# VectorE's general path rolled into a loop, and its flag made earlier

## The chip, the cores and the metric

One core of one Trainium2 chip runs the kernel. The metric is the device time of one execution in microseconds; the kernel before takes 160.34 us (median of 3 runs, 160.16 to 160.55).

## What is computed

For each of 128 graphs with 128 nodes and 128 features, `x` holds the node features and `adj` the integer kind of each edge. Two layers follow each other:

```python
# layer 1; rels(a, r) is (a == r) as 0.0 or 1.0
h = x @ W.T
vals_r = (h + b_r) * sigmoid(h @ Wg.T + bg_r)       # W, Wg, b, bg for each way
y = sum(rels(adj, r) @ vals_r for r in 2..40)       # forward
y += sum(rels(adj.T, r) @ vals_r for r in 2..40)    # backward
y += rels(adj.T, 1) @ vals_1                        # loop
x = layernorm(x + relu(y))
# layer 2
y = sum(rels(adj, r) @ x @ weight[r] for r in 1..4) + bias
x = layernorm(x + y)
```

The drawn `adj` holds only 0 and 1. So of the 40 relations of layer 1 and the 4 of layer 2 only relation 1 has edges.

## The kernel before

**The fast path.** It takes `adj` to be 0 or 1 everywhere. The 128 graphs are 32 groups of four. Each group is one tile of 128 x 512, and a software pipeline runs over the groups. TensorE projects (`project`), sums over neighbours (`loop_sum`), forms the messages (`messages`) and multiplies them by the weight (`message_weights`). ScalarE seeds PSUM, takes the sigmoid, copies messages, scales the second norm's outputs and looks at every tile of `adj` (`look`, whose sums land in `seen_sum`). VectorE forms the products and residual sums and the moments of both norms. GpSimd applies the first norm and takes inverse roots of variances by a power. SP (SyncE) issues loads of `x` and its transpose and all stores. GpSimd issues the loads of `adj` and its transpose.

**The tail.** The last five groups, `LAST` = 27 to `LAST + 4` = 31, are written out by hand below the loops (lines 1075 to 1106 for VectorE, 601 to 615 for TensorE, 771 to 782 for ScalarE, 433 to 439 for GpSimd, 323 to 332 for SP). On VectorE the order of calls in that list is the order of the work. A variance made by `last_variance(q)` (L905) releases a power on GpSimd (L410). That power releases the scaling of group q by ScalarE (L716) or by VectorE (`last_norm2`, L1015), and the scaled tile releases SP's store (L301). The last group is handled in halves (`half_...`; variances L984, powers L405).

**The flag.** `find_odd` reduces `seen_sum` (L1020) and compares (L1023). Its comparison gives one value per partition, which says whether an edge kind other than 0 and 1 was seen. TensorE adds these over partitions with a matmul against ones (L614), and VectorE copies the sum as an integer to `flag` (L1103). VectorE's reduction stands behind the statistics of group `LAST + 2`, TensorE's matmul behind all other matmuls, and the copy just ahead of the last variance.

**The general path.** Every engine ends with `general` (L272): it waits for `flag_ready`, loads the flag into a register (L274) and branches (L275). With the flag at 0 it jumps over the whole general path. Only with a flag above 0 would it compute everything again, for any `adj`, in 16 pairs of groups. For this input each engine waits, loads, compares and jumps. SP then waits at L353 until all stores have landed, and all engines meet at the end (L80).

The general path of TensorE and of ScalarE already has a loop over the two groups of a pair. That of VectorE is written out twice, by a Python `for` at L1141:

```python
            def general_pair(pair):
                dve.wait_ge(gadj_in, (pair + 1) * 32)
                for half_ in range(2):
                    g = pair * 2 + half_
```

Of the kernel before, what the change touches and what calls it, by code (L numbers as in the profile page):

```python
# [5 lines left out]
F32 = mybir.dt.float32  # L6
# [3 lines left out]
ALU = mybir.AluOpType  # L10
# [3 lines left out]
P = 128  # L14
B = 128
GB = 4
# [3 lines left out]
EPS = 1e-5  # L20
# [32 lines left out]
FWD, BWD, LOOP = range(3)  # L53
RSQRT_MAGIC = float(0x5F3759DF)
NEWTON = 3
CHAIN = 1 + 2 * (1 + 5 + 3 * NEWTON)


def exists(q):
# [18 lines left out]
def build(nc, x, x_t, adj, adj_t, w_in, w_loop_t, wg_loop_t, gate_bias, consts,  # L78
          w_rel_t, wg_rel_t, b_rel, bg_rel, w_msgs, rel_ids, out):
    with ExitStack() as ctx:  # L80
        def sb(name, shape, dt):
            return ctx.enter_context(nc.sbuf_tensor(name, shape, dt))
# [61 lines left out]
        gsum = sb("gsum", [P, W], F32)  # L144
        gx1 = sb("gx1", [P, W], F32)
        gmsg = sb("gmsg", [P, GB, MSGS * P], F32)
        gstat = sb("gstat", [P, GB, 6], F32)
        gmv = sb("gmv", [P, GB, 2], F32)
        gtiny = sb("gtiny", [P, 4, GB], F32)
        worst = sb("worst", [P, 1], F32)  # L150
        odd = sb("odd", [P, 1], F32)
# [92 lines left out]
        def half_columns(p):  # L244
            return slice(2 * p * P, 2 * (p + 1) * P)
# [14 lines left out]
        def batch(b):  # L260
            return slice(b * P, (b + 1) * P)
# [189 lines left out]
        def _(pe):  # L451
# [105 lines left out]
            def inject(q):  # L557
                pe.wait_ge(consts_in, 16)
                await_x1(q)

                pe.wait_ge(vals_done, q + 1)
                for b in range(GB):
                    nc.tensor.matmul(y_of(q, b, 1), ident, x1[:, q % X1_RING, batch(b)],
                                     start=b == 0, stop=False, skip_group_check=True)

            def message_weights(q):
                if exists(q):
                    if q == 0:
                        pe.wait_ge(w1_mid, 6)

                    if q in INJECTED:
                        pe.wait_ge(vals_done, q + 1)
                    else:
                        await_count(pe, z_done, q)
                    pe.wait_ge(msgt_done, q + 1)
                    for b in range(GB):
                        last = nc.tensor.matmul(y_of(q, b, 1), msg_t[:, q % 2, batch(b)], w1[:, :],  # L577
                                                start=q not in INJECTED, stop=True,
                                                skip_group_check=q in INJECTED)
                    last.then_inc(y_done, 1)  # L580

            for t in range(GROUPS):
# [20 lines left out]
            message_weights(GROUPS - 3)  # L603
            messages(GROUPS - 2)
            inject(GROUPS - 2)
            message_weights(GROUPS - 2)
            half_messages(0)
            half_messages(1)
# [1 line left out]
            half_message_weights(0)  # L610
            half_inject(1)
            half_message_weights(1)
            pe.wait_ge(odd_ready, 2)
            nc.tensor.matmul(aux_ps[0:1, 2 * P:2 * P + 1], odd[:, :], ones[:, :], start=True, stop=True)\  # L614
                .then_inc(odd_count, 1)

            def relation(step, ways):
                pe.wait_ge(rel_vals, step)
# [201 lines left out]
        def _(dve):  # L820
# [137 lines left out]
            def half_variance1(p):  # L958
                q = GROUPS - 1
                dve.wait_ge(bn1_done, q + 1 + p)  # L960

                dve.wait_ge(nmr_done, q - 1)
                m2 = stats[:, q % STATS_RING, p, :].rearrange("p (i k) -> p i k", k=3)[:, :, 2]
                ts(var1[:, q % 2, 2 * p:2 * p + 2], m2, 1.0 / P, EPS, ALU.mult, ALU.add).then_inc(mean_done, 1)
# [21 lines left out]
            def second_sum(q):  # L986
                dve.wait_ge(y_done, q + 1)
                dve.wait_ge(x1_done, q + 1)

                await_count(dve, out_done, q - Z_RING + 1)  # L990
                tt(z_sb[:, q % Z_RING, :], y_ps[:, :], x1[:, q % X1_RING, :], ALU.add).then_inc(z_done, 1)  # L991
# [89 lines left out]
            half_first_stats(1)  # L1081
            second_stats(LAST + 1, 1)
            half_variance1(1)
            second_sum(LAST + 2)
            last_variance(LAST + 1)
            half_norm1(0)
            second_stats(LAST + 2, 0)
            half_norm1(1)
            second_stats(LAST + 2, 1)
            odd_steps = find_odd()  # L1090
            next(odd_steps)
            second_stats(LAST + 3, 0)
            last_variance(LAST + 2)
            next(odd_steps, None)
            second_stats(LAST + 3, 1)
            last_norm2(LAST + 2, (0, 1))
            last_variance(LAST + 3)
# [1 line left out]
            last_norm2(LAST + 2, (2, 3))  # L1099
            half_variance2(0)  # L1100
            second_stats(LAST + 4, 1)
            dve.wait_ge(odd_count, 1)
            nc.vector.tensor_copy(flag[:, :], aux_ps[0:1, 2 * P:2 * P + 1]).then_inc(flag_ready, 1)  # L1103
            half_variance2(1)
            last_norm2(LAST + 4, (0, 1))
            last_norm2(LAST + 4, (2, 3))
# [1 line left out]
            def vals_and_masks(step, half_, ways, r, number):  # L1108
                dve.wait_ge(rel_gates, step)
                for way in ways:  # L1110
                    source = LOOP if r is None else way
                    column = bass.ds(2 * RELS if r is None else r + way * RELS, 1)
                    stt(gvals_t[:, way, :], gh[:, source, :], gb[:, column], ggate[:, way, :], ALU.add, ALU.mult)
                for way in ways:
                    edges = adjt_sb[:, half_, :] if way == FWD else adj_sb[:, half_, :]
                    last = ts(gmask[:, way, :], edges, number, None, ALU.is_equal)
                last.then_inc(rel_vals, 1)

            def normalise(dst, src, chain):
                var, y, yy, w = (gtiny[:, i, :] for i in range(4))  # L1120
                for b in range(GB):
                    last = nc.vector.bn_stats(gstat[:, b, :], src[:, batch(b)])
                chain(last)
                nc.vector.tensor_copy(worst[:, :], ones[:, :])
                for b in range(GB):
                    last = nc.vector.bn_aggr(gmv[:, b, :], gstat[:, b, :])
                chain(last)
                chain(ts(var, gmv[:, :, 1], EPS, None, ALU.add))
                chain(ts(y.bitcast(I32), var.bitcast(I32), -0.5, RSQRT_MAGIC, ALU.mult, ALU.add))
                for _ in range(NEWTON):  # L1130
                    chain(tt(yy, y, y, ALU.mult))
                    chain(stt(w, yy, -0.5, var, ALU.mult, ALU.mult))
                    chain(stt(y, w, 1.5, y, ALU.add, ALU.mult))
                for b in range(GB):
                    last = ts(dst[:, batch(b)], src[:, batch(b)], gmv[:, b, 0:1], y[:, b:b + 1],
                              ALU.subtract, ALU.mult)
                chain(last)

            def general_pair(pair):
                dve.wait_ge(gadj_in, (pair + 1) * 32)  # L1140
                for half_ in range(2):  # L1141
                    g = pair * 2 + half_
                    steps = [0]

                    def chain(ins):
                        steps[0] += 1
                        ins.then_inc(gchain, 1)
                        dve.wait_ge(gchain, g * CHAIN + steps[0])

                    first = g * (RELS + 1) + 1  # L1150
                    vals_and_masks(first, half_, (BWD,), None, 1.0)
                    dve.wait_ge(rel_product, first)
                    nc.vector.tensor_copy(gsum[:, :], bank[3]).then_inc(rel_added, 1)
                    with dve.Fori(0, RELS) as r:
                        vals_and_masks(first + 1 + r, half_, (FWD, BWD), r, gids[:, bass.ds(r, 1)])
                        dve.wait_ge(rel_product, first + 1 + r)
                        tt(gsum[:, :], bank[3], gsum[:, :], ALU.add).then_inc(rel_added, 1)
                    dve.wait_ge(rel_added, first + RELS)
                    dve.wait_ge(gx_in, (g + 1) * 32)
                    chain(stt(gsum[:, :], gsum[:, :], 0.0, x_sb[:, 0, :], ALU.max, ALU.add))  # L1160
                    normalise(gx1, gsum, chain)
                    for k in range(MSGS):
                        last = ts(gmask[:, k, :], adjt_sb[:, half_, :], float(k + 1), None, ALU.is_equal)
                    last.then_inc(gmasks_ready, 1)
                    dve.wait_ge(gy_done, g + 1)
                    chain(tt(gsum[:, :], y_ps[:, :], gx1[:, :], ALU.add))
                    for b in range(GB):
                        last = tt(gsum[:, batch(b)], gsum[:, batch(b)], b1, ALU.add)
                    chain(last)
                    normalise(out_sb[:, 0, :], gsum, chain)  # L1170
                    assert steps[0] == CHAIN
                    nc.vector.tensor_copy(worst[:, :], ones[:, :]).then_inc(gout_ready, 1)
                    dve.wait_ge(gout_st, (g + 1) * 16)

            general(dve, general_pair)


# [46 lines left out]
```

## Time and profile before

| | us |
|---|---|
| median of 3 runs | 160.34 |
| profiled execution | 159.43 |
| its span in the trace | 157.3 |
| PE, DVE, ACT, POOL busy | 149.0, 138.5, 128.1, 113.5 |

The span runs from the first to the last instruction of the trace. The profiled execution's own time is 2.1 us longer, and lies 0.9 us under the median of the unprofiled runs. PE is TensorE, DVE VectorE, ACT ScalarE, POOL GpSimd and SP SyncE. A name with a q behind it is that engine's sequencer: it handles waits, register loads, branches and DMA issues. Durations of single instructions are in ns, all other times in us.

### The profile page before, as it was taken

The numbers are of one execution on the slowest core, as the hardware profiler recorded it, in microseconds if no ns is written. First come the engines' busy times: TensorE is split into PE (matmuls) and PEld (weight loads), VectorE is DVE, ScalarE is ACT, GpSimd is POOL, SyncE is SP. The second block draws the span as 40 slices with busy tenths as digits, with TensorE's granted clock in tenths as the row PEclk, the third lists the DMA queues.
The fourth block names the chain that finished last, engine by engine and source line by source line (L and its number), as shares of the span: only waits on it lengthen the run. The fifth ranks groups of instructions, "written<-read, shape, count | busy, mean of one in ns | idle before, by whom it ended". The sixth has DMA issues, their size and how long they took to land.

```text
span 157.3 us, 3862 instructions
## 1 busy us (share of the span) xinstructions
PE 149.0 (95%) x1055; PEld 138.7 (88%) x1055; DVE 138.5 (88%) x567; ACT 128.1 (81%) x293; POOL 113.5 (72%) x221
## 2 busy tenths in 40 slices
PE   6999999999999999999999999999999999999920
PEld 3698999999999999999999999999999999999920
DVE  1459599799999999999999999999999999999870
ACT  3579888769888888889988888889988888869940
POOL 1318878847877778779877778778877776867760
PEclk9999999999999999999999999999999999999996
DMA  3999999997899998999899999999989862341243
GB/s 129 307 391 400 403 395 391 404 312 247 234 310 277 295 287 300 311 301 321 284 292 311 308 290 277 305 276 299 323 308 295 250 206 77 108 162 67 109 164 140
DMA packets 19320, 42.75 MB, mean 272 GB/s; under 512 B 2144, under 2 KB 2784, under 8 KB 19296
## 3 DMA queue, kind: packets, MB, share of 16 engines
q1 hardware_dynamic: 14400, 25.76, 48.2%
q0 software_dynamic: 4608, 16.52, 32.9%
q8 instruction: 9, 0.15, 0.4%
q10 hardware_dynamic: 288, 0.20, 0.4%
q14 instruction: 15, 0.12, 0.2%
HBM read 34.08 MB, written 8.39 MB: 270 GB/s over the span
## 4 chain that ended last, share of the span: by engine, by line
PE 80%; DMA 5%; DVE 4%; issue 3%; SPq 2%; POOL 2%; POOLq 0%; DVEq 0%
PE hg_ps L473 31%; PE loop_ps L488 17%; PE msg_ps L553 16%; PE y_ps L577 16%; DMA xt_sb<-x_t_dram 5%; POOL last_rstd L410 1%; SPq L293 1%; DVE last_stats L1004 1%; POOL last_rstd L405 1%; PE aux_ps L553 1%; SPq L298 1%; DVE x L974 1%; DVE s_sb L948 0%; DVE out_sb L1015 0%; DVE z_sb L991 0%
## 5 line engine op out<-in xcount | busy, mean ns | idle before, releaser
L473 PE MATMUL hg_ps<-w_all,xt_sb 128*128 128x256 f32 x256 | 60.8, 381 | 0.2
L388 POOL TENSOR_SCALAR x<-s_sb,rstd,nmr 128x128 f32<-128x128 f32 x114 | 49.7, 448 | 3.3
L473 PEld LDWEIGHTS hg_ps<-w_all,xt_sb 128*128 128x128 f32 x256 | 46.2, 190 | 6.0 <-DMA xt_sb<-x_t_dram 0.8
L379 POOL TENSOR_TENSOR rstd<-var,power 128x4 f32<-128x4 f32 x31 | 32.0, 1033 | 20.9 <-DVE var L913 18.4
L716 ACT ACTIVATE out_sb<-z_sb,rstd 128x128 f32<-128x128 f32 x108 | 36.9, 392 | 0.5 <-DVE rstd L885 0.5
L674 ACT ACTIVATE hg_ps<-gate_b 128x1024 f32<-128x1024 f32 (+1 forms) x32 | 31.9, 1000 | 2.6 <-DVE vals L921 1.9
L683 ACT ACTIVATE gate<-hg_ps 128x512 f32<-128x512 f32 x32 | 19.0, 595 | 17.5 <-PE hg_ps L473 17.5
L488 PE MATMUL loop_ps<-vals,adj_sb 128*128 128x128 f32 x248 | 33.0, 276 | 0.2
L577 PEld LDWEIGHTS y_ps<-w,msg_t 128*128 128x128 f32 x240 | 31.3, 191 | 1.5
L577 PE MATMUL y_ps<-w,msg_t 128*128 128x128 f32 x240 | 31.8, 275 | 0.0
L488 PEld LDWEIGHTS loop_ps<-vals,adj_sb 128*128 128x128 f32 x248 | 30.5, 192 | 0.7 <-issue 0.5
L553 PE MATMUL msg_ps<-adjt_sb,x 128*128 128x128 f32 x232 | 30.7, 275 | 0.0
L553 PEld LDWEIGHTS msg_ps<-adjt_sb,x 128*128 128x128 f32 x232 | 28.2, 192 | 0.2 <-DMA adjt_sb<-adj_t_dram 0.2
L931 DVE SCALAR_TENSOR_TENSOR s_sb<-loop_ps,x_sb 128x512 f32<-128x512 f32 x31 | 21.4, 689 | 6.3 <-PE loop_ps L488 3.2
L936 DVE BATCH_NORM_STATS2 stats<-s_sb 128x6 f32<-128x256 f32 x62 | 25.5, 427 | 0.0
L1004 DVE BATCH_NORM_STATS2 stats<-z_sb 128x6 f32<-128x256 f32 x54 | 22.9, 427 | 0.0
L921 DVE TENSOR_TENSOR vals<-hg_ps,gate 128x512 f32<-128x512 f32 x32 | 21.7, 680 | 1.2 <-ACT gate L683 1.2
L741 ACT ACTIVATE seen<-adj_sb,half 128x512 bf16<-128x512 f32 x32 | 22.7, 710 | 0.0
L991 DVE TENSOR_TENSOR z_sb<-y_ps,x 128x512 f32<-128x512 f32 x30 | 20.4, 680 | 1.1 <-PE y_ps L577 1.1
L693 ACT ACTIVATE msg_t<-msg_ps 128x512 f32<-128x512 f32 x29 | 16.8, 580 | 0.0
L362 POOL DMA_DIRECT2D adj_sb<-adj_dram x15 | 9.3, 623 | 4.7 <-DMA xt_sb<-x_t_dram 2.6
L369 POOL DMA_DIRECT2D adjt_sb<-adj_t_dram x16 | 10.1, 631 | 0.0
(93 smaller groups left out, 119.8 us busy)
## 6 DMA issues: line engine op xcount, KB each, us to landing
xt_sb<-x_t_dram SPq DMA_DIRECT2D x32, 256.0 KB, 4.2
x_sb<-x_dram SPq DMA_DIRECT2D x32, 256.0 KB, 4.2
adjt_sb<-adj_t_dram POOLq DMA_DIRECT2D x16, 512.0 KB, 5.1
out<-out_sb SPq DMA_DIRECT2D x32, 256.0 KB, 3.3
adj_sb<-adj_dram POOLq DMA_DIRECT2D x15, 512.0 KB, 5.2
raw<-adj_dram SPq DMA_DIRECT2D x1, 256.0 KB, 3.7
adj_sb<-adj_dram POOLq DMA_DIRECT2D x1, 256.0 KB, 5.8
const_sb<-consts_dram SPq DMA_DIRECT2D x1, 192.0 KB, 6.2
```

What stands on the lines that cost most here:

```text
L379: nc.gpsimd.tensor_tensor(r, var1[:, q % 2, :], power[:, :], ALU.pow).then_inc(rstd1_done, 1)
L388: done = nc.gpsimd.tensor_scalar(x1[:, q % X1_RING, batch(b)], s_sb[:, q % S_RING, batch(b)], r[:, b:b + 1], n[:, b:b + 1], ALU.mult, ALU.add)
L473: last = nc.tensor.matmul(hg_ps[:, q % 2, b, :], xt_sb[:, q % XT_RING, batch(b)], w_gate, start=False, stop=True, skip_group_check=True)
L488: last = nc.tensor.matmul(loop_ps[:, batch(b)], adj_sb[:, spot, batch(b)], vals[:, q % 2, batch(b)], start=True, stop=True)
L553: last = nc.tensor.matmul(msg_of(q)[:, batch(b)], x1[:, q % X1_RING, batch(b)], adjt_sb[:, spot, batch(b)], start=True, stop=True)
L577: last = nc.tensor.matmul(y_of(q, b, 1), msg_t[:, q % 2, batch(b)], w1[:, :], start=q not in INJECTED, stop=True, skip_group_check=q in IN ...
L674: nc.scalar.activation(hg_ps[:, q % 2, 0:graphs, :], gate_b[:, None, :].broadcast_to([P, graphs, 2 * P]), ACT.Copy).then_inc(seeded, 1)
L716: last = nc.scalar.activation(out_sb[:, q % OUT_RING, batch(b)], z, ACT.Copy, scale=r)
L741: nc.scalar.activation(seen[:, :], adj_sb[:, 2 * spot + q % 2, :], ACT.Square, bias=half[:, 0:1], accum_out=seen_sum[:, q:q + 1]).then_inc ...
L921: tt(vals[:, q % 2, :].rearrange("p (b n) -> p b n", b=GB), hg_ps[:, q % 2, :, 0:P], gate[:, q % 2, :].rearrange("p (b n) -> p b n", b=GB) ...
L936: got = nc.vector.bn_stats(stats[:, q % STATS_RING, p, :], s_sb[:, q % S_RING, 2 * p * P:2 * (p + 1) * P].rearrange("p (i n) -> p n i", i=2))
L1004: got = nc.vector.bn_stats(into, z.rearrange("p (i n) -> p n i", i=2))
```

## The change

On VectorE the two groups of the general path become a loop in the instruction stream, and `normalise` takes statistics of two interleaved graphs per instruction, drops the aggregation and adds the bias in one instruction. In all VectorE's general path has 111 instructions for 231. None of these runs for this input.

In the tail, the reduction goes right behind `half_variance1(1)`, the last variance of the first norm, and the comparison behind `second_sum(LAST + 2)`. TensorE's matmul for the flag goes between `inject(GROUPS - 2)` and `message_weights(GROUPS - 2)`, and VectorE's copy to `flag` behind `half_norm1(1)`. Scratch tiles of the general path shrink.

```diff
@@ TensorE
             messages(GROUPS - 2)
             inject(GROUPS - 2)
+            pe.wait_ge(odd_ready, 2)
+            nc.tensor.matmul(aux_ps[0:1, 2 * P:2 * P + 1], odd[:, :], ones[:, :], start=True, stop=True)\
+                .then_inc(odd_count, 1)
             message_weights(GROUPS - 2)
...
             half_message_weights(1)
-            pe.wait_ge(odd_ready, 2)
-            nc.tensor.matmul(aux_ps[0:1, 2 * P:2 * P + 1], odd[:, :], ones[:, :], start=True, stop=True)\
-                .then_inc(odd_count, 1)
@@ VectorE
             half_variance1(1)
+            odd_steps = find_odd()
+            next(odd_steps)
             second_sum(LAST + 2)
+            next(odd_steps, None)
             last_variance(LAST + 1)
             half_norm1(0)
             second_stats(LAST + 2, 0)
             half_norm1(1)
+            dve.wait_ge(odd_count, 1)
+            nc.vector.tensor_copy(flag[:, :], aux_ps[0:1, 2 * P:2 * P + 1]).then_inc(flag_ready, 1)
             second_stats(LAST + 2, 1)
-            odd_steps = find_odd()
-            next(odd_steps)
             second_stats(LAST + 3, 0)
             last_variance(LAST + 2)
-            next(odd_steps, None)
             second_stats(LAST + 3, 1)
...
             second_stats(LAST + 4, 1)
-            dve.wait_ge(odd_count, 1)
-            nc.vector.tensor_copy(flag[:, :], aux_ps[0:1, 2 * P:2 * P + 1]).then_inc(flag_ready, 1)
             half_variance2(1)
@@ VectorE, general path (jumped over)
             def general_pair(pair):
-                dve.wait_ge(gadj_in, (pair + 1) * 32)
-                for half_ in range(2):
+                with dve.Fori(0, 2) as half_:
+                    dve.wait_ge(gadj_in, (pair + 1) * 32)
                     g = pair * 2 + half_
...
             def normalise(dst, src, chain):
                 var, y, yy, w = (gtiny[:, i, :] for i in range(4))
-                for b in range(GB):
-                    last = nc.vector.bn_stats(gstat[:, b, :], src[:, batch(b)])
+                for p in range(2):
+                    last = nc.vector.bn_stats(gstat[:, p, :],
+                                              src[:, half_columns(p)].rearrange("p (i n) -> p n i", i=2))
                 chain(last)
-                nc.vector.tensor_copy(worst[:, :], ones[:, :])
-                for b in range(GB):
-                    last = nc.vector.bn_aggr(gmv[:, b, :], gstat[:, b, :])
-                chain(last)
-                chain(ts(var, gmv[:, :, 1], EPS, None, ALU.add))
+                m = gstat[:, :, :].rearrange("p c (i k) -> p (c i) k", k=3)
+                chain(ts(var, m[:, :, 2], 1.0 / P, EPS, ALU.mult, ALU.add))
...
-                    for b in range(GB):
-                        last = tt(gsum[:, batch(b)], gsum[:, batch(b)], b1, ALU.add)
-                    chain(last)
+                    by_graph = gsum[:, :].rearrange("p (b n) -> p b n", b=GB)
+                    chain(tt(by_graph, by_graph, b1[:, None, :].broadcast_to([P, GB, P]), ALU.add))
```

## Rows read from the trace of the kernel before

**Rows 1.** The page's chain that ended last, shares of the span by engine.

```profile
PE 80%; DMA 5%; DVE 4%; issue 3%; SPq 2%; POOL 2%; POOLq 0%; DVEq 0%
```

**Rows 2.** SP's stores (L301): the issue at 153.4, landings of 153:154, 152:153, 147:152.

```profile
L301 SPq DMA_DIRECT2D out<-out_sb x1: 1752/1752/1752, 153.4 to 153.4; - x1
DMA to landing us min/median/max: 3.5/3.5/3.5
...
DMA to landing us min/median/max: 3.7/3.7/3.7
...
DMA to landing us min/median/max: 2.0/2.0/2.0
```

**Rows 3.** Instruction fetches by queue (packets, MB, share): 153.1:153.4, 153.42:153.5, 154.6:154.75, 107.4:107.6.

```profile
q8 instruction: 1, 0.02, 35.1%
...
q14 instruction: 1, 0.01, 59.9%
...
q14 instruction: 1, 0.01, 16.6%
...
q8 instruction: 1, 0.02, 29.4%
```

**Rows 4.** SP's queue, packets, MB and share of 16 engines in 150:152.

```profile
q1 hardware_dynamic: 162, 0.30, 40.4%
```

**Rows 5.** SP's load issue (L293) and store issue (L301) in 107:109.

```profile
L293 SPq DMA_DIRECT2D xt_sb<-x_t_dram x1: 1202/1202/1202, 107.6 to 107.6; - x1
...
L301 SPq DMA_DIRECT2D out<-out_sb x1: 344/344/344, 107.2 to 107.2; - x1
```

**Rows 6.** L274 and L275: TensorE's load of the flag, branches of three engines.

```profile
L274 PEldq TENSOR_LOAD <-flag x1: 693/693/693, 151.5 to 151.5; - x1
...
L275 ACTq COMPARE_BRANCH  x1: 50/50/50, 152.4 to 152.4; - x1
L275 PEldq COMPARE_BRANCH  x1: 237/237/237, 152.7 to 152.7; - x1
...
L275 DVEq COMPARE_BRANCH  x1: 72/72/72, 153.7 to 153.7; - x1
```

**Rows 7.** The meeting at the end, L80: VectorE's drain.

```profile
L80 DVEq DRAIN  x1: 59/59/59, 156.6 to 156.6; - x1
```

**Rows 8.** Timeline of VectorE: start, duration, instruction.

```profile
145.63 0.15 DVE L964 TENSOR_SCALAR var<-stats 128x2 f32<-128x2 f32 x1
...
148.05 0.17 DVE L1020 TENSOR_REDUCE worst<-seen_sum 128x1 f32<-128x32 f32 x1
148.14 0.42 DVE L1004 BATCH_NORM_STATS2 last_stats<-hg_ps 128x6 f32<-128x256 f32 x1
148.48 0.15 DVE L905 TENSOR_SCALAR last_var<-last_stats 128x4 f32<-128x4 f32 x1
148.54 0.15 DVE L1023 TENSOR_SCALAR odd<-worst 128x1 f32<-128x1 f32 x1
148.60 0.42 DVE L1004 BATCH_NORM_STATS2 last_stats<-hg_ps 128x6 f32<-128x256 f32 x1
...
151.35 0.13 DVE L1103 CAST flag<-aux_ps 1x1 int32<-1x1 f32 x1
151.47 0.17 DVE L984 TENSOR_SCALAR last_var<-last_stats 128x2 f32<-128x2 f32 x1
```

**Rows 9.** Timeline of GpSimd from 148.7, idle time and its releaser in brackets.

```profile
148.71 1.01 POOL L410 TENSOR_TENSOR last_rstd<-last_var,power 128x4 f32<-128x4 f32 x1 [1.11 <-DVE last_var L905]
150.39 1.01 POOL L410 TENSOR_TENSOR last_rstd<-last_var,power 128x4 f32<-128x4 f32 x1 [0.68 <-DVE last_var L905]
151.37 1.36 POOL L405 TENSOR_TENSOR last_rstd<-last_var,power 128x2 f32<-128x2 f32 x2
```

**Rows 10.** Timeline of ScalarE's last look and of TensorE's last groups of matmuls.

```profile
144.91 0.19 ACT L741 ACTIVATION_READ_ACCUMULATOR seen<-adj_sb,half 128x1 f32 x1
...
149.78 0.61 PE L531 MATMUL hg_ps<-w,msg_t 128*128 128x128 f32 x4
150.32 0.19 PE L614 MATMUL aux_ps<-ones,odd 128*1 128x1 f32 x2
```

More of the change, by code:

```diff
@@ L55 @@
 NEWTON = 3
-CHAIN = 1 + 2 * (1 + 5 + 3 * NEWTON)
+CHAIN = 1 + 2 * (1 + 4 + 3 * NEWTON)
 def exists(q):
@@ L146, in build @@
         gmsg = sb("gmsg", [P, GB, MSGS * P], F32)
-        gstat = sb("gstat", [P, GB, 6], F32)
-        gmv = sb("gmv", [P, GB, 2], F32)
+        gstat = sb("gstat", [P, 2, 6], F32)
         gtiny = sb("gtiny", [P, 4, GB], F32)
@@ L1114, in vals_and_masks @@
                 for way in ways:
-                    edges = adjt_sb[:, half_, :] if way == FWD else adj_sb[:, half_, :]
-                    last = ts(gmask[:, way, :], edges, number, None, ALU.is_equal)
+                    edges = (adjt_sb if way == FWD else adj_sb)[:, bass.ds(half_, 1), :]
+                    last = ts(gmask[:, way, :], edges.rearrange("p o n -> p (o n)"), number, None, ALU.is_equal)
                 last.then_inc(rel_vals, 1)
@@ L1134, in normalise @@
                 for b in range(GB):
-                    last = ts(dst[:, batch(b)], src[:, batch(b)], gmv[:, b, 0:1], y[:, b:b + 1],
+                    last = ts(dst[:, batch(b)], src[:, batch(b)], m[:, b, 1:2], y[:, b:b + 1],
                               ALU.subtract, ALU.mult)
@@ L1161, in general_pair @@
                     normalise(gx1, gsum, chain)
+                    edges = adjt_sb[:, bass.ds(half_, 1), :].rearrange("p o n -> p (o n)")
                     for k in range(MSGS):
-                        last = ts(gmask[:, k, :], adjt_sb[:, half_, :], float(k + 1), None, ALU.is_equal)
+                        last = ts(gmask[:, k, :], edges, float(k + 1), None, ALU.is_equal)
                     last.then_inc(gmasks_ready, 1)
@@ L1173, in general_pair @@
                     dve.wait_ge(gout_st, (g + 1) * 16)
+                    nc.vector.tensor_copy(worst[:, :], ones[:, :])
             general(dve, general_pair)
```

## The prediction

> **What bounds the kernel now.** The page's chain comes first. It runs for 80% of the span through TensorE's matmuls [rows 1]. The change touches none of these; all of it lies behind 145.6 us of a span of 157.3. So I read the tail, from the end backwards. The last thing to happen is the landing of the last store: issued at 153.40, landed 3.5 us later, at 156.9, and the meeting of the engines ends 0.4 us behind that. The reader should see two oddities in the rows of the stores [rows 2]. The last issue occupied SP for 1752 ns, and the two last stores took 3.7 and 3.5 us to land where the four before them took 2.0. So the tail holds about 1.5 us that is neither computing nor a store's ordinary time.
>
> The queues say what stood there [rows 3]. A share of 16 engines turned back into the time of one packet (35.1% of 16 x 0.30 us) gives 1.68 us for a fetch of 16 KB of instructions that began between 153.1 and 153.4; one of 8 KB at 153.42 to 153.50 took 59.9% of 16 x 0.08 = 0.77 us, and one of 8 KB at 154.60 to 154.75 took 0.40 us. They follow the jumps over the general path [rows 6]: TensorE branches at 152.7 and the 16 KB fetch begins 0.4 us later; ScalarE at 152.4 and VectorE at 153.7, and an 8 KB fetch begins 1.0 us after each. I take these three pairings as right; nothing but the times ties them.
>
> That a 16 KB fetch holds SP's issue is seen once more [rows 3, 5]. A store was issued at 107.2, a fetch of 29.4% of 16 x 0.2 = 0.94 us began behind 107.4, and the next issue, at 107.6, took 1202 ns. It ended near 108.8, some 0.3 us behind the fetch. At the end it is the same: the fetch over at about 154.85, the issue at 153.40 + 1.75 = 155.15. The pattern is one earlier DMA caught on the fetch's engine, then the next issue held until 0.3 us after the fetch.
>
> VectorE shows a second stall: it branches at 153.7 and drains at 156.6 [rows 6, 7], 2.85 us with a fetch between. It is hidden at present, since the store's landing at 156.9 is later.
>
> What leads to the last issue at 153.40 is an alternation of VectorE and GpSimd [rows 8, 9]. GpSimd waited 1.11 us for VectorE's variance of 148.48, ran 1.01 us, and VectorE's scaling and next variance followed; the power of 150.39 and the two halves from 151.37 (1.36 us) run back to back. VectorE has no idle time from 145.6 to 149.0. Whatever is added to it ahead of 148.48 moves the last issue by the same amount.
>
> **The change part by part.** *The reduction.* It leaves the place ahead of 148.48, where it cost 0.09 us from start to start (148.05 to 148.14), and comes back at 145.7, before that same variance [rows 8]. Net 0. Its wait for the last look is over: that ended at 145.10 [rows 10], 0.6 us earlier.
>
> *The comparison.* It stood behind 148.48 and comes ahead of it: +0.06 us (148.54 to 148.60) [rows 8].
>
> *The copy of the flag.* It cost 0.12 us from start to start (151.35 to 151.47) at a place where GpSimd, not VectorE, set the pace: the second half's variance came at 151.47 and GpSimd was busy with the first half until about 152.05 [rows 8, 9]. So its going gives nothing, and its coming ahead of 148.48 costs up to 0.12; part of that gap may have been the wait of L984, so from 0.04. The sum on VectorE is +0.10 to +0.18; I take 0.17. At full durations, with nothing overlapping, it would be 0.17 + 0.15 + 0.13 - 0.09 = 0.36 us, the upper bound. The lower bound is +0.06. No gain is possible here, as nothing leaves that path but the reduction's own 0.09.
>
> *The wait in front of the copy.* Behind it are queued the statistics of `LAST + 2` and all that follows, with GpSimd waiting. The comparison is over at about 146.5, TensorE's matmul of 0.19 us [rows 10] by about 146.8, and the copy comes at about 147.9, behind the first norm's second half. Cover 1.1 us, cost nothing.
>
> *TensorE's matmul.* It is placed in a busy stretch, ahead of the weights of group 30, and costs 0.1 to 0.2 us there (0.19 in all, and up to 0.1 of waiting for the comparison). The last matmuls then end at about 150.55 instead of 150.39 [rows 10]. VectorE reads them behind the scaling of `LAST + 2`, at 151.01 before and 151.18 now. Cover 0.6 us; it costs nothing.
>
> *The earlier flag.* It is ready at about 148.0 instead of 151.48. ScalarE, GpSimd, VectorE and SP meet their flag loads only behind their own last work, so for them it changes little: ScalarE's jump comes about 0.1 us later. TensorE alone was waiting for it: its last matmuls start at 149.78 and its load at 151.5, directly behind the flag [rows 6, 10]. It can now load at about 150.2, jump at about 151.4, and fetch its 16 KB from 151.85 on. With 0.94 to 1.68 us for the fetch [rows 3], that ends between 152.8 and 153.55. Before, it ended at 154.85.
>
> What is late next? The last issue starts at 153.40 + 0.17 = 153.57. It meets no 16 KB fetch, so the 1.42 us by which it was held (1752 against the 333 to 344 ns of a free issue, one of which is in [rows 5]) go. In the worst case the issue before it, due at 152.77, is held to 153.85, which puts the last one 0.3 us back. With all quiet the store would land at 153.57 + 2.0 = 155.6. But ScalarE's 8 KB fetch stays, at about 153.56. One DMA engine comes free of it between 153.96 (at 0.40 us) and 154.33 (at 0.77 us) with two stores' shares behind it. One share is 8 packets at 40.4% of 32 us over 162 = 80 ns, 0.64 us [rows 4]. From the end of the 16 KB fetch at 154.84 to the landing of the store that it caught (152.60 + 3.7 = 156.3) passed 1.46 us. So two shares land 1.46 + 0.64 = 2.1 us after that engine is free: 156.1 to 156.4. I take 156.2 against 156.86. The span falls by about 0.7 us, to 156.6.
>
> *The shorter general path.* It removes no executed instruction. What it changes is how far VectorE jumps. VectorE's drain must come earlier than 156.6, or it becomes the next bound. The fetches in these rows are 8 KB each on that queue; a jump over 231 instructions went past what had been fetched, and one over 111 should fall within it. If so the drain comes at about 154.0, and the fetch that a jump into the next block starts (0.40 us) runs beside the stores, nobody waiting. I count 0 for it, and it is the cover for the rest.
>
> The Trainium skill speaks against this last step. Its page "Runtime: NRT & Kernel Launch", section "Instruction fetch mechanics", has blocks of 16 KiB, 256 instructions, with two of them in reach of a jump without a stall. By that rule a jump over 231 instructions never leaves the window, VectorE's 2.85 us would have another cause, and the rolled loop would not move them. The case of that rule is the second rival below.
>
> **The sum.** +0.17 on VectorE, -1.42 for the held issue, +0.55 for the backlog behind ScalarE's fetch: -0.7 us. The profiled execution's 159.43 becomes 158.7. It lies 0.9 under the median of the runs; applied to that median, 160.34 becomes 159.65.
>
> **The rivals.** *All of it comes back.* The 8 KB fetch catches no engine that matters, because it runs 0.4 us or less and ahead of the packets. The store lands at 155.6, -1.25 us: 159.1. For it speaks that a fetch behind 154.6 took only 0.40 us; against it that the one beside stores took 0.77.
>
> *VectorE's drain still stalls.* Its 2.85 us stay, it drains at 156.6 + 0.17 = 156.75, and the meeting ends at 156.97, for 157.3 before: -0.35, 160.0. For it: the fetch landed near 155.1 and VectorE went on only at 156.6, so more than the fetch may be in it. Against it: the other engines, with shorter code, drained at once.
>
> *The tail stays held.* The 8 KB fetches or the remaining ones hold the last issue as before, or TensorE's fetch does not follow its jump; only +0.17 is left: 160.5, no change that can be told. For it: two 8 KB fetches still lie beside the last stores.
>
> *Slower.* The tail stays held and the flag's three instructions cost VectorE what they last, +0.36: 160.7. The place is VectorE's stretch from 145.6 to 148.5, and it decides from an added 0.32 us with nothing released. For it: VectorE has no gap there, and the copy reads PSUM after a wait. Against it: overlapped neighbours in [rows 8] show start-to-start gaps of 0.06 and 0.09.
>
> **How the numbers follow.** The forecast 0.42, everything back 0.14, VectorE's stall 0.14, held tail 0.19, slower 0.11. What a measurement of this kernel can tell from no change is about 0.2%, 0.32 us. The first two cases are faster; of VectorE's stall, at -0.35, I count two thirds as faster; of the held tail nearly all is no change. That gives 0.66 faster, 0.22 the same, 0.12 slower. The range of eight in ten goes from full relief, 159.1, to the held tail, 160.5, and I leave a tenth of a microsecond of run-to-run spread below. The forecast's own range is 159.3 to 159.9.
>
> **What would show it.** Right: TensorE's flag load near 150.2 and a 16 KB fetch beginning near 151.9; the last issue at 153.5 to 153.6, lasting about 333 ns; the last landing near 156.2 and one increment late; VectorE's drain within 0.5 us of its branch. GpSimd's power of 148.71 should come 0.10 to 0.18 us later. Wrong: a last issue over 1 us long, a power later by more than 0.3 us, or VectorE still idle for 2 us behind its branch.

## The result, and the profile after

The changed kernel takes 159.31 us (median of 7 runs, 158.79 to 159.40). The kernel before, run beside it, takes 160.16 us (158.94 to 160.88). The ratio is 0.9936, with a 95% interval from 0.9908 to 0.9965: 0.64% faster, about 1.0 us. Run twice more it gave 0.9921 (0.9890 to 0.9952) and 0.9926 (0.9910 to 0.9942), so 1.2 us is nearer the truth than 1.0. The forecast was 159.65, 0.7 us faster. The ratios leave out executions more than 1.5% above a kernel's fastest.

The two profiled spans are both 157.3 us long, and nothing in them says "faster" until the head is set apart. The last variance of the first norm (L964 before, L963 after) comes at 145.63 before [rows 8] and at 146.54 after. It stands ahead of everything that the change moves, the code's length apart. In this execution TensorE stood 1.4 us for its second load near the start:

```profile
8.47 1.99 PE L472 MATMUL hg_ps<-w_all,xt_sb 128*128 128x256 f32 x8 [1.38 <-DMA xt_sb<-x_t_dram]
```

Over 14 traces of these kernels, one execution each, that variance starts anywhere from 145.4 to 147.0. So all tails below are counted from it, and I call it the anchor. VectorE's timeline after:

```profile
146.54 0.15 DVE L963 TENSOR_SCALAR var<-stats 128x2 f32<-128x2 f32 x1
146.60 0.18 DVE L1019 TENSOR_REDUCE worst<-seen_sum 128x1 f32<-128x32 f32 x1
...
147.29 0.14 DVE L1022 TENSOR_SCALAR odd<-worst 128x1 f32<-128x1 f32 x1
147.35 0.21 DVE L904 TENSOR_SCALAR last_var<-last_stats 128x4 f32<-128x4 f32 x1
...
148.78 0.14 DVE L1092 CAST flag<-aux_ps 1x1 int32<-1x1 f32 x1
148.85 0.41 DVE L1003 BATCH_NORM_STATS2 last_stats<-z_sb 128x6 f32<-128x256 f32 x1
```

The comparison costs 0.06 us from start to start (147.29 to 147.35) and the copy 0.07 (148.78 to 148.85). GpSimd's timeline shows what arrives of that:

```profile
149.74 1.01 POOL L409 TENSOR_TENSOR last_rstd<-last_var,power 128x4 f32<-128x4 f32 x1 [1.09 <-DVE last_var L904]
151.42 1.01 POOL L409 TENSOR_TENSOR last_rstd<-last_var,power 128x4 f32<-128x4 f32 x1 [0.67 <-DVE last_var L904]
```

The power starts 3.20 us behind the anchor, where before it started 3.08 behind it (148.71 - 145.63, [rows 9]): the early flag costs 0.12 us. The flag load of TensorE, the branches and VectorE's drain come next:

```profile
L273 PEldq TENSOR_LOAD <-flag x1: 490/490/490, 150.2 to 150.2; - x1
...
L274 PEldq COMPARE_BRANCH  x1: 374/374/374, 151.1 to 151.1; - x1
L274 ACTq COMPARE_BRANCH  x1: 50/50/50, 153.2 to 153.2; - x1
...
L274 DVEq COMPARE_BRANCH  x1: 72/72/72, 154.7 to 154.7; - x1
...
L80 DVEq DRAIN  x1: 63/63/63, 155.3 to 155.3; - x1
```

TensorE loads the flag 3.65 us behind the anchor, for 5.9 before [rows 6], and while its last matmuls still run. VectorE drains 0.6 us behind its branch; before it was 2.9 [rows 6, 7]. The instruction fetches, in the stretches 152.1 to 152.3 and 154.2 to 154.4, and the stores issued at 151.3, 153.6 and 154.4 with their landings:

```profile
q8 instruction: 1, 0.02, 44.0%
...
q14 instruction: 1, 0.01, 14.1%
```

```profile
L300 SPq DMA_DIRECT2D out<-out_sb x1: 332/332/332, 151.3 to 151.3; - x1
DMA to landing us min/median/max: 3.7/3.7/3.7
...
L300 SPq DMA_DIRECT2D out<-out_sb x1: 332/332/332, 153.6 to 153.6; - x1
DMA to landing us min/median/max: 2.6/2.6/2.6
...
L300 SPq DMA_DIRECT2D out<-out_sb x1: 332/332/332, 154.4 to 154.4; - x1
DMA to landing us min/median/max: 2.4/2.4/2.4
```

The 16 KB fetch (44.0% of 16 x 0.2 = 1.41 us) begins 1.1 us behind TensorE's branch and is over just ahead of the issue of 153.6. It now makes the stores of 151.3 and 152.1 late (3.7 and 3.5 us), for which nobody waits. The last issue is free at 332 ns [rows 2 had 1752], and its store lands 2.4 us later instead of 3.5.

From the anchor, in us, read from the traces:

| | last issue | last landing | VectorE drains | end |
|---|---|---|---|---|
| before | 7.8 | 11.2 | 10.95 | 11.7 |
| after | 7.9 | 10.3 | 8.7 | 10.8 |

So the tail is 0.9 us shorter in the profiles, near what the runs say, and the equal spans come from the head.

### The profile page after: what moved, and what is told of

The parts are those of the page before. It is cut to its first block, busy times and chain, and to the rows that moved or that the text cites. A ratio compares the mean times of both kernels' runs of the same rounds, so it can differ in the third digit from the quotient of the medians.

```text
span 157.3 us, 3862 instructions
## 1 busy us (share of the span) xinstructions
PE 148.7 (95%) x1055; PEld 138.5 (88%) x1055; DVE 138.4 (88%) x567; ACT 128.2 (81%) x293; POOL 113.5 (72%) x221
## 4 chain that ended last, share of the span: by engine, by line
PE 84%; DVE 4%; DMA 4%; issue 3%; POOL 2%; SPq 1%; POOLq 0%; DVEq 0%
PE hg_ps L472 33%; PE loop_ps L487 18%; PE y_ps L576 16%; PE msg_ps L552 16%; DMA xt_sb<-x_t_dram 4%; POOL last_rstd L409 1%; DVE last_stats L1003 1%; POOL last_rstd L404 1%; PE aux_ps L552 1%; DVE x L973 1%; DVE s_sb L947 0%; DVE out_sb L1014 0%; DVE z_sb L990 0%; DVE stats L935 0%; SPq L306 0%
## 5 line engine op out<-in xcount | busy, mean ns | idle before, releaser
L472 PE MATMUL hg_ps<-w_all,xt_sb 128*128 128x256 f32 x256 | 60.8, 380 | 1.4 <-DMA xt_sb<-x_t_dram 1.4
```

Of the source, the lines that this page charges most:

```text
L472: last = nc.tensor.matmul(hg_ps[:, q % 2, b, :], xt_sb[:, q % XT_RING, batch(b)], w_gate, start=False, stop=True, skip_group_check=True)
```

## The experiments

Each edit is against the kernel named; every ratio is to the kernel before, run beside it on the same chip. Experiments 1 to 4 ran together on one chip, 5 to 7 on another, and 8, with the first extra trace of experiment 3, on the first chip again. Code is shown in excerpts, cut where `...` stands. All positions are in us behind each trace's own anchor unless a time of the trace is quoted.

### 1. The order alone

The kernel before with the four moves of the diff (TensorE's matmul, the reduction, the comparison, the copy). VectorE's general path stays whole, with 231 instructions. Against the kernel before, VectorE's part:

```diff
             half_variance1(1)
+            odd_steps = find_odd()
+            next(odd_steps)
             second_sum(LAST + 2)
+            next(odd_steps, None)
...
             half_norm1(1)
+            dve.wait_ge(odd_count, 1)
+            nc.vector.tensor_copy(flag[:, :], aux_ps[0:1, 2 * P:2 * P + 1]).then_inc(flag_ready, 1)
...
```

> The order of the changed kernel (flag made early), with VectorE's general path still written out twice, 231 instructions to jump over. Times are counted from the last variance of the first norm (second L964 in the trace of before). There the last store is issued at 7.8 us, lands at 11.2 and the span ends at 11.7; in the changed kernel 7.9, 10.3 and 10.7. Theory: the early jump of TensorE frees the last store, so its issue is 333 ns long and it lands near 10.3; but VectorE jumps past what was fetched, drains 2.9 us behind its branch, at about 11.0, and sets the end: span to 11.2, and 0.4 to 0.5 us faster than before, half of the whole gain. Rival (the length of the jump does not matter): VectorE drains 0.6 us behind its branch and all of the gain, 0.9 to 1.0 us, is there.

Measured: ratio 0.9997 (0.9970 to 1.0024), no change. The last store's issue (153.4) and landing, then VectorE's branch and drain; this trace's anchor is 145.50:

```profile
L301 SPq DMA_DIRECT2D out<-out_sb x1: 333/333/333, 153.4 to 153.4; - x1
DMA to landing us min/median/max: 2.4/2.4/2.4
...
L275 DVEq COMPARE_BRANCH  x1: 72/72/72, 153.6 to 153.6; - x1
...
L80 SPq DRAIN  x1: 7/7/7, 156.1 to 156.1; - x1
L80 DVEq DRAIN  x1: 58/58/58, 157.1 to 157.1; - x1
```

The theory had the shape right. The last store is free and lands at 10.3; SP is done at 10.6. VectorE drains last, at 11.55 behind the anchor, and sets the end. But it drains 3.4 us behind its branch and not 2.9, so in this trace nothing is left of the expected 0.4 to 0.5 us; the interval of the times reaches just that far (0.9970 is 0.5 us) and does not settle it. The rival, that the general path's length does not matter, is out: it asked for 0.9 to 1.0 us.

### 2. The rolled path alone

The changed kernel with its tail put back into the order of the kernel before (the four moves of the diff undone).

> VectorE's rolled general path alone, with the flag made as late as in the kernel before. Theory: VectorE drains within 0.7 us of its branch instead of 2.9, but the last store's issue is still held for over 1 us and its landing sets the end, 11.7 us behind the anchor: no change, within 0.1 us of before. Rival (VectorE's stall was the bound): faster by 0.5 us or more.

Measured: ratio 0.9958 (0.9928 to 0.9988), 0.7 us faster, with times from 158.34 to 160.54. The theory expected nothing and fell; the rival's "0.5 us or more" came. The profile is of an execution at 159.90, in the upper half of these times; anchor 145.66. The last two stores, VectorE's branch, and the drains of VectorE and SP:

```profile
L300 SPq DMA_DIRECT2D out<-out_sb x1: 332/332/332, 152.6 to 152.6; - x1
DMA to landing us min/median/max: 4.1/4.1/4.1
...
L300 SPq DMA_DIRECT2D out<-out_sb x1: 332/332/332, 153.4 to 153.4; - x1
DMA to landing us min/median/max: 3.9/3.9/3.9
...
L274 DVEq COMPARE_BRANCH  x1: 72/72/72, 153.7 to 153.7; - x1
...
L80 DVEq DRAIN  x1: 63/63/63, 154.3 to 154.3; - x1
L80 SPq DRAIN  x1: 7/7/7, 157.6 to 157.6; - x1
```

VectorE is done at once. The 16 KB fetch falls at 8.1 behind the anchor, later than in the first profile (7.5), and does not hold the issue at all; instead one part of each of the last two stores comes 1.9 to 2.1 us late. The end is at 12.1, later than in the profile of before. So the lateness of the store is not one figure: it depends on where the fetch falls in an execution. That in the faster executions of this kernel it falls where it costs nothing is inferred from their times; none of them was traced. Experiment 3 traces both kinds, for another kernel.

### 3. TensorE's jump held back

The changed kernel, with one wait on TensorE ahead of its flag load.

```diff
+            pe.wait_ge(last_var_done, 6)
             general(pe, general_pair)
```

> The changed kernel, with one wait added on TensorE ahead of its flag load, for VectorE's last variance, so that TensorE jumps as late as in the kernel before; nothing else changes. Theory: TensorE's 16 KB fetch falls on the last stores again, the last issue takes over 1 us, and the end comes 11.7 to 11.8 us behind the anchor: as before or 0.1 us slower. Rival (the gain comes from VectorE's end of the tail: no copy of the flag there, a short jump): it stays as fast as the changed kernel, 0.9 to 1.0 us under before, and the issue is free.

Measured: ratio 0.9965 (0.9935 to 0.9995), 0.6 us faster than before, about half of the changed kernel's gain. Neither answer of the expectation came: of 12 times six lie from 158.72 to 158.98 and six from 159.72 to 160.66, with none between. The profile was of the lower group (158.98), with the 16 KB fetch 4.2 us behind the anchor although TensorE branched at 7.3. Two more executions of the same kernel were traced to see whether the groups are the two places of the fetch.

> A second look at the changed kernel with TensorE's jump held back. Its 12 times fell into two groups, near 158.8 and near 160.1 us, and the one profile was of the lower group with the 16 KB fetch at 4.2 us behind the anchor, ahead of the last stores. Theory: in executions of the upper group the fetch comes at 7.5 us or later and the last store lands 1 to 1.5 us later; so this look is either (fetch near 4.2, end near 10.6, time near 158.8) or (fetch at 7.5 to 9, end near 11.7 to 12.1, time near 160.1). Rival: a time near 160.1 with the fetch early, or near 158.8 with it late.

> A third look at the changed kernel with TensorE's jump held back, since the second look was of the lower group (159.01 us, 16 KB fetch at 4.2 us behind the anchor, end at 10.7). Theory: a time near 160.1 goes with a fetch at 7.5 us or later and an end at 11.7 to 12.1; a time near 158.9 goes with a fetch near 4.2 and an end near 10.7. Rival: any other pairing.

The second trace is of 159.01 us, the third of 160.60. First the second (anchor 146.11): its last store, TensorE's branch, and the 16 KB fetch in 150.25 to 150.4:

```profile
L300 SPq DMA_DIRECT2D out<-out_sb x1: 333/333/333, 154.0 to 154.0; - x1
DMA to landing us min/median/max: 2.3/2.3/2.3
...
L274 PEldq COMPARE_BRANCH  x1: 248/248/248, 153.4 to 153.4; - x1
...
q8 instruction: 1, 0.02, 44.8%
```

Then the third (anchor 146.64), the fetch in 155.5 to 155.7:

```profile
L300 SPq DMA_DIRECT2D out<-out_sb x1: 333/333/333, 154.5 to 154.5; - x1
DMA to landing us min/median/max: 3.5/3.5/3.5
...
L274 PEldq COMPARE_BRANCH  x1: 368/368/368, 153.9 to 153.9; - x1
...
q8 instruction: 1, 0.02, 30.0%
```

It is the same program. In one execution the fetch comes ahead of TensorE's wait, at 4.2, and the end is at 10.7; in the other it follows the jump, at 9.0, the last store lands 1.2 us later, and the end is at 11.85. The times pair with the places as the theory said, in three traces of three. What holding TensorE back costs is the chance of the late place: 1.2 us, in about half of the executions if the twelve times are read by these three traces.

Beside experiment 2 this shows something more. Both kernels have the rolled path and both jump late; they differ in where the flag's steps stand. Their ratios, taken together on one chip, are 0.9958 and 0.9965. So the order by itself gives nothing that can be told, and what is left, up to the changed kernel's 0.9921, is put down to TensorE's early jump. The intervals of 0.9965 and 0.9921 overlap a little; the two groups of times are the stronger evidence.

### 4. The changed kernel again

> The changed kernel once more, beside these three on the same chip: 0.8 to 1.1 us faster than before; last issue 7.9 us behind the anchor and 333 ns long, landing near 10.3, end near 10.7.

Measured: 0.9921 (0.9890 to 0.9952), times from 158.61 to 159.92. Last issue 7.9, landing 10.5, end 11.0; the fetch at 5.6. The landing and the end are 0.2 to 0.3 us later than expected. The issue before the last took 452 ns, until 0.36 us behind the fetch.

### 5. TensorE's general path cut short

TensorE's body of the general path is replaced by one wait (this leaves out TensorE's share of the general path, which this input never enters). First on the kernel before, then on the kernel of experiment 2.

```diff
             def general_pair(pair):
-                with pe.Fori(0, 2) as half_:
...
-                    last.then_inc(gy_done, 1)
+                pe.wait_ge(flag_ready, 1)
```

> The kernel before with TensorE's general path cut to an empty loop (it leaves out TensorE's share of the general path, which this input never enters), so that TensorE's jump is short and should need no 16 KB fetch; flag and jumps stay late, VectorE's general path stays at 231 instructions. Theory A (the end is the later of two nearly equal things, the last store's landing and VectorE's drain, and each change alone leaves the other): the last store is issued free and lands 9.8 to 10.3 us behind the anchor, VectorE drains at 11.0 to 11.6 and ends the span at 11.3 to 11.8: within 0.3 us of before. Rival B (the last store alone set the end): 0.9 us faster or more. Rival C (the 16 KB fetch does not hold anything): the last two stores land as late as in before, 10.6 and 11.2.

> The same cut of TensorE's general path, together with VectorE's rolled general path, and the flag as late as in before. Theory A: both late things are gone; last issue at 7.8, landing 9.8 to 10.2, end 10.3 to 10.7 behind the anchor; 1.0 to 1.3 us faster than before, at least as fast as the changed kernel, as the 0.1 us that the early flag costs VectorE is not paid. Rival D (the rolled loop is the whole gain, TensorE's fetch adds nothing): as the rolled loop alone, 0.4 to 0.7 us under before. Rival E (the early flag itself is needed): no faster than the rolled loop alone.

Measured: 0.9980 (0.9957 to 1.0004) and 0.9939 (0.9902 to 0.9977). The cut was to take the 16 KB fetch away and did so in neither kernel. In the first (anchor 146.95) the fetch fell at 4.4, ahead of the last two stores, so that its trace shows a tail with free stores all the same:

```profile
L301 SPq DMA_DIRECT2D out<-out_sb x1: 333/333/333, 154.7 to 154.7; - x1
DMA to landing us min/median/max: 2.6/2.6/2.6
...
L80 SPq DRAIN  x1: 7/7/7, 157.5 to 157.5; - x1
L80 DVEq DRAIN  x1: 58/58/58, 158.4 to 158.4; - x1
```

The store landed at 10.35, but VectorE drained at 11.40 and ended the span at 11.7: VectorE's stall alone gives the tail of before. That is theory A; that the fetch fell early in this trace was luck. The second kernel is less clear than its ratio, which rests on seven of its 12 times. Its 12 times are three from 158.16 to 158.49, three near 159.6 and six from 160.53 to 161.10; the median of all is 160.11, no better than before (160.04). In the profile (159.57, anchor 145.83) the fetch came at 7.5, 0.4 us behind TensorE's branch, in 153.3 to 153.5:

```profile
q8 instruction: 1, 0.02, 34.7%
...
L300 SPq DMA_DIRECT2D out<-out_sb x1: 1223/1223/1223, 153.6 to 153.6; - x1
DMA to landing us min/median/max: 3.4/3.4/3.4
```

So the edit failed as a test of a tail without fetch, and it gave something else: the held issue once more. The fetch took 34.7% of 3.2 = 1.11 us and ended 8.64 behind the anchor; the issue ended at 9.0, again 0.3 to 0.4 us behind it. In these traces a fetch at 7.5 holds the last issue; one at 8.1 or later does not hold it but delays one part of the last store or of the last two, which costs as much or more. Rivals B and C of the first expectation are out. D and E of the second are not settled by this kernel, and why half of its times lie above the median of before is not known.

### 6. The kernel before again

> The kernel before once more, for a second look at its tail. Theory A: same time within the noise of 0.2 to 0.3%; VectorE drains 2.9 to 3.4 us behind its branch, at 11.0 to 11.6 behind the anchor, and the last store lands at 10.9 to 11.6, either of them ending the span. Rival (the first look was typical): VectorE drains at 10.95 and the store at 11.2 alone ends it.

Measured: 0.9992 (0.9972 to 1.0013); the profile is of an execution at 161.20 (anchor 146.80). Last store, VectorE's branch and drain:

```profile
L301 SPq DMA_DIRECT2D out<-out_sb x1: 333/333/333, 154.6 to 154.6; - x1
DMA to landing us min/median/max: 4.1/4.1/4.1
...
L275 DVEq COMPARE_BRANCH  x1: 72/72/72, 154.8 to 154.8; - x1
...
L80 DVEq DRAIN  x1: 57/57/57, 158.2 to 158.2; - x1
```

VectorE drains 3.4 us behind its branch, at 11.4; the store lands at 11.8, with the fetch at 8.8, and the end is at 12.3. So in both traces of this kernel the store ended the span, but here VectorE alone would have ended it at 11.7. Neither trace is typical: this one is of the slowest of its 12 executions, and the first had the shortest of the four stalls seen with 231 instructions (2.9, 3.4, 3.4, 3.4) and a held issue that did not come back here.

### 7. ScalarE's jump moved within its block

The changed kernel with a small copy on ScalarE ahead of 26 of its sigmoids.

```diff
+                if t > 5:
+                    nc.scalar.activation(pad[:, :], half[:, :], ACT.Copy)
                 gates(t)
```

> The changed kernel with one copy of a 128x1 tile put ahead of each of ScalarE's sigmoids from the sixth group on, 26 in all, where ScalarE waits for TensorE anyway, so that the jump of ScalarE no longer leads into a new 8 KB block of its instructions. Theory: the 8 KB fetch 7.7 us behind the anchor is gone from there (it comes 2 to 4 us earlier), the last store lands after 2.0 us instead of 2.4, at 9.9 behind the anchor, end at 10.35: 0.3 to 0.5 us faster than the changed kernel. Rival: the copies delay the sigmoids and cost more than they give, or the landing stays 2.4 us because of TensorE's fetch or VectorE's.

Measured: 0.9917 (0.9888 to 0.9945), 158.82 us. The profile does as expected: in this trace (anchor 145.89) the last store lands after its quiet 2.0 us, and the 8 KB fetch is at 4.35 behind the anchor, in the stretch 150.2 to 150.3:

```profile
L301 SPq DMA_DIRECT2D out<-out_sb x1: 332/332/332, 153.8 to 153.8; - x1
DMA to landing us min/median/max: 2.0/2.0/2.0
...
q14 instruction: 1, 0.01, 19.3%
```

The end is at 10.4, against 10.7 to 11.0 in three traces of the changed kernel. That the fetch at 7.7 moved when only ScalarE's code grew also shows that it was ScalarE's. In the times the step is not shown: 0.9917 beside the changed kernel's 0.9921 and 0.9926, measured at other times.

The trace shows a third late thing. GpSimd's drain takes 2691 ns in all 14 traces and here ends at 10.13, with SP's at 10.17:

```profile
L80 POOLq DRAIN  x1: 2691/2691/2691, 153.3 to 153.3; - x1
...
L80 SPq DRAIN  x1: 7/7/7, 156.1 to 156.1; - x1
```

So a store that landed still earlier would gain next to nothing.

### 8. Both, and the copy in VectorE's idle time

```diff
-            dve.wait_ge(odd_count, 1)
-            nc.vector.tensor_copy(flag[:, :], aux_ps[0:1, 2 * P:2 * P + 1]).then_inc(flag_ready, 1)
             second_stats(LAST + 2, 1)
             second_stats(LAST + 3, 0)
             last_variance(LAST + 2)
+            dve.wait_ge(odd_count, 1)
+            nc.vector.tensor_copy(flag[:, :], aux_ps[0:1, 2 * P:2 * P + 1]).then_inc(flag_ready, 1)
```

On top of experiment 7 (its copies are not shown again).

> The changed kernel with ScalarE's 26 small copies, and with the copy of the flag put behind VectorE's last_variance(LAST + 2), where VectorE then waits for GpSimd, instead of behind half_norm1(1). Theory: only the comparison's 0.06 us is left ahead of that variance, so GpSimd's power for LAST + 2 starts 3.14 us behind the anchor (3.20 in the changed kernel, 3.08 before) and the last store is issued at 7.83 and lands at 9.9; the end comes at 10.3 against 10.8 to 11.0 in the changed kernel, so 0.4 to 0.6 us faster than the changed kernel and 1.4 us faster than before. Rival: the flag comes later for TensorE, whose 16 KB fetch then touches the last stores, and nothing is gained over the changed kernel.

> The changed kernel beside it, for the comparison: 0.6 to 1.1 us faster than before; TensorE's fetch at 4.3 to 5.7 us behind the anchor, before the last two stores are issued; end at 10.6 to 11.0; its times spread over less than the kernel before's.

Measured: 158.66 us (158.16 to 158.90), ratio 0.9919 (0.9902 to 0.9935); the changed kernel beside it 158.82 us (158.60 to 158.94), 0.9926 (0.9910 to 0.9942). GpSimd's power starts at 148.58, 3.14 behind the anchor of 145.44, as expected, and the last issue comes at 7.84. But the last store took 2.3 us and not 2.0, and the end is at 10.6. It is the lowest median of all, by 0.16 us, but the ranges overlap: a gain over the changed kernel is not shown.

## Why the prediction was right, and where it was off

**The early flag's cost: right.** 0.12 us against 0.17 taken, within 0.10 to 0.18. The copy cost 0.07 us where [rows 8] had 0.12. I had left open that part of that gap was the wait of L984; that fits, and no run shows it.

**TensorE jumps earlier, and that frees the last issue: right, and more than I said.** The load comes even earlier than forecast (3.65 behind the anchor for 4.6), as TensorE's sequencer reaches it while the matmuls run. The fetch came at 5.6, 5.6 and 4.2 in three traces of the changed kernel (forecast 6.2, and 0.4 us behind the branch; it was 1.1 behind it twice and once ahead of it), and at 4.8, 4.3 and 4.2 in the other three kernels with an early jump. With late jumps it was seen at 4.2, 4.2, 4.4, 7.5, 7.5, 8.1, 8.8 and 9.0. I had taken the 16 KB fetch as one event that follows the jump. It falls in different places in different executions of one program, and only those at 7.5 or later made the last store land more than 2.6 us behind its issue. So the term of -1.42 us, the held issue, was there in one trace of before and not in the other, where a freely issued store took 4.1 us to land. In none of six traces with an early jump did the fetch come later than 5.6. The spread of times agrees: 158.60 to 159.92 in 19 runs of the changed kernel.

**The backlog behind ScalarE's fetch: right in kind, a little large.** I took 2.6 us from issue to landing (153.57 to 156.2). It was 2.4, 2.6 and 2.4 in the three traces. Experiment 7 moved the fetch away and the landing was 2.0. Experiment 8 moved it too, and the last store took 2.3: one of its 16 parts came 0.3 us behind the others, with another 8 KB fetch (0.31 us, from 9.54) beside it.

**VectorE's jump: the step that was mis-sized.** The prediction said of the rolled path "I count 0 for it, and it is the cover for the rest". The direction was right: with 111 instructions VectorE drains 0.6 us behind its branch in all ten traces (I had asked for 0.5), with 231 after 2.9 to 3.4 in all four. But the one profile had the shortest stall seen, with which VectorE alone would have ended the span at 11.2, 0.5 us ahead of the store. In the other three traces with 231 instructions it drains at 11.4 to 11.55, and in two of them that ends the span, at 11.7 and 11.8, though the store has long landed. That such a floor lay under most executions of the kernel before is inferred; it fits experiments 1 and 5, whose traces have an early landing and whose times are those of before. Hence the order alone gave nothing that can be told (experiment 1), the rolled path alone 0.4% (experiment 2), and the two together 0.6 to 0.8%, about 1.2 us and not 0.7. The end went from 11.7 and 12.3 in two traces to 10.7 to 11.0 in three.

So the sum came near in part by luck. It gave all of its 0.7 us to the earlier flag and none to the shorter path. By the experiments the flag alone gives 0.0, the path alone 0.7, and only both together 1.2.

**The sum** was then -0.7 against a measured -0.85 between the medians and -1.0 by the ratio. The range held it. With the two repeats, the gain is 1.2 us and the sum is half a microsecond short. The rival "VectorE's drain still stalls" did not come; priced from the typical stall it would have been no gain at all, as experiment 1 shows, and not the 0.35 us that I gave it.

**The rule of the Trainium skill.** Two blocks of 16 KiB in reach, from the Trainium skill's page "Runtime: NRT & Kernel Launch" ("Instruction fetch mechanics"), would have kept VectorE from stalling over 231 instructions. The trace disagrees: the queue that serves VectorE and ScalarE (q14) fetches instructions 8 KB at a time, and the stall is there with 231 and gone with 111. The measurement decides. VectorE's drain comes 1.5 us behind the end of such a fetch in all four traces with the stall, whether the fetch begins 1.0 or 1.6 us behind the branch; that difference is the whole one between 2.9 and 3.4. No run changes the length of the path and nothing else in it: that the distance decides, and not where the blocks end or how the path is written, is the simplest reading and not separately shown.

**Still open.** Why the 16 KB fetch falls in different places in executions of the same program. It is settled in part before the tail begins: in the five traces where the fetch came 1.1 to 1.8 us behind TensorE's branch, the fetch before it on that queue had come 3.9 to 4.4 us ahead of the anchor; in the nine others 5.6 to 6.2 ahead, and then the last one came at 4.2 to 4.8 (seven) or at 7.5 (two). Open too is what the 1.5 us between the end of VectorE's fetch and its drain consist of [rows 3, 7], and whether TensorE's fetch could be kept out of the tail altogether, since cutting its path did not do it.

## What to carry to other kernels

A branch at the end of a kernel can cost more than its own instructions. Here VectorE's jump over 231 instructions held it for about 3 us, one over 111 did not, and instruction fetches fell on the last stores. Keep skipped code short and let engines jump before the last stores are issued; here it took both to get the whole gain. Where two late things end within half a microsecond of each other, trace several executions before calling one of them the bound. Count tails from an instruction just ahead of the change, since the head alone moved by 1.5 us over these traces.

## What the runs showed of the hardware that was not expected

- The 16 KB instruction fetch of TensorE's queue (q8) took 0.96 to 1.69 us in the tail, and began 4.2 to 9.0 us behind the same instruction in executions of kernels that differ little or not at all. The ten stores issued 0.07 to 1.2 us ahead of its start landed 3.1 to 4.2 us after their issue instead of 2.0.
- SP's issue was held by it for 1752, 1223 and 1202 ns, in each case until 0.3 to 0.4 us behind the fetch, when an earlier DMA was already caught. The same end, 0.36 to 0.37 us behind the fetch, marks four shorter holds in the tails of other traces (552, 452, 383 and 353 ns), and 0.38 us the longest hold in any of the traces, 2387 ns at 60.8 in the third trace of experiment 3. Where the fetch began 0.36 us or more behind the start of the last issue, that issue stayed at 332 or 333 ns.
- TensorE's branch took 368 or 374 ns in all five traces where the fetch followed it by 1.1 us or more, and 237 to 252 ns where the fetch came before it or closer behind it.
